# Another order for the first loads, splits and products of a Perceiver block on one Trainium2 core

## The chip, the core and the metric

The kernel runs on one core of one Trainium2 chip. The metric is the time of one execution on the device in microseconds (us), here the median of several runs.

## What is computed

The inputs are x (64 sequences of 64 rows, 256 wide) and a context (64 sequences of 256 rows, 256 wide). One block is applied to x:

```python
x = x + xattn(layernorm(x), ctx, ctx, Wq, bq, Wk, bk, Wv, bv, Wo, bo)   # 16 heads of 16
x = x + attn(layernorm(x), w_qkv, b_qkv, w_out, b_out)                  # causal, 16 heads
x = x + ffn(layernorm(x), w_gate, w_up, w_down)                         # quantized silu(gate)*up, inner 1024
```

In the cross attention, the only part that the change touches, `q = queries @ Wq.T + bq`, `k = keys @ Wk.T + bk`, `v = values @ Wv.T + bv`, then softmax of `q k / 4` over the 256 keys, times v, times Wo.

## The kernel before

Two sequences (2 x 64 rows of x) make one tile of 128 rows; there are 32 tiles, t = 0 to 31, and each has two contexts s = 0 and 1, one for each of its sequences. The program is written by hand for each engine, with semaphores between them. An engine runs its own list strictly in order, so the place of an instruction in its list decides what waits behind it. Three stages follow one another: cross attention for all tiles (to about 560 us), causal self attention, feed forward. The change lies ahead of the first loop of the first stage and in the first pass of it.

Products that need accuracy are split: a float32 matrix is copied to its float32r rounding ("h") by ScalarE, and the remainder ("l") is formed by a subtraction. The product is then three float32r products, h by h, h by l and l by h, each over two halves of the 256 inner values. So a key or value projection of one context is 12 matmuls of 128x256.

The pieces, by name and line:

- `pe_xt` (L269 to L275): two transposes of the normalized tile `xn` by TensorE. `act_xt` (L466 to L470) copies the result to `xnT` and rounds it to `x1h`; `pool_xl1` (L513 to L517) forms `x1l`.
- `pe_q` (L277 to L286): queries of two tiles at once, 12 matmuls whose moving side is 256 columns wide (2 x 128 rows of x). `dve_q` (L415 to L424) adds the bias and masks by head into `qb`, four instructions.
- `act_c` and `pool_c` split a context into `ch` and `cl`. `pe_k` (L288) and `pe_v` (L301) project it; `dve_k` (L410) and `dve_v` (L405) take the results out of PSUM and add the bias.
- `pe_scores` (L317) makes the scores of one context, 8 float32 matmuls on 32 rows each. `dve_max` (L456) takes the row maxima, `act_exp` (L492) the eight exponentials, `pe_transpose` (L335) 16 transposes of the probabilities, and `pe_pv` (L353) the product with the values. `pool_rm` and `pe_r` (L346) bring the reciprocal sums into place.
- `dve_stats` and `dve_xn` (L380 to L403) are the layer norm; POOL's `pool_rstd` (L511) sits between them. `pool_xb` (L519 to L522) adds the output bias to x into `x_all`.
- The weights `wk`, `wv`, `wq` are split once at the start: ScalarE makes `wkh`, `wvh`, `wqh` (L1472 to L1477), VectorE `wkl`, `wvl`, `wql` (L1309 to L1316).

SyncE's queue issues the loads of x and of the contexts. In `body(t)` it waits for `xn_done` t + 1 and `xb_done` t + 1 before it loads the x of tile t + 2, and behind that, in order, come the contexts of tile t + 1:

```python
sp_.wait_ge(xn_done, t + 1)
sp_.wait_ge(xb_done, t + 1)
sp_.dma_start(x_sb[j][:], x_v[bass.ds(t + 2, 1)].rearrange(
```

VectorE's `body(0)` begins with `dve_stats` of tile 2, which waits for that x. GpSimd's list at the start (L1594 to L1603) is `pool_rstd(0)`, `pool_c(0, 0)`, `pool_rstd(1)`, `pool_xl1(0)`, `pool_xl1(1)`, `pool_c(0, 1)`, `pool_xb(0)`, `pool_xb(1)`. ScalarE's `act_exp(0, 0)` stands behind `act_xt(1)` and `act_c(0, 1)` (L1478 to L1480).

Of the kernel before, what the change touches and what calls it, by code (L numbers as in the profile page):

```python
# [44 lines left out]
def block_kernel(nc, x, ctx_t, wq, bq, wk, bk, wv, bv, wo, bo, w_qkv, b_qk, b_v2, w_out, b_out,  # L45
# [8 lines left out]
    with ctx:  # L54
# [128 lines left out]
        wk_in = sem("wk_in")  # L183
        wv_in = sem("wv_in")
# [9 lines left out]
        SET_Q = [(wq_sb[:], k_of(wq)), (bq_sb[:], bq), (bk_sb[:], bk), (qm_sb[:], q_mask)]  # L194
# [23 lines left out]
        q_mm = sem("q_mm")  # L218
        qb_done = sem("qb_done")
# [36 lines left out]
        xt1_ps = mp[:, 0:D].rearrange("p (k t) -> p k t", k=KT)  # L256
# [12 lines left out]
        def pe_xt(pe, t, to):  # L269
            pe.wait_ge(xn_done, t + 1)  # L270
            if not isinstance(t, int) or t > 2:
                pe.wait_ge(y_ev, t - 2)
            for k in range(KT):
                last = nc.tensor.transpose(to[:, k, :], xn[:, k * P:(k + 1) * P], id_sb[:])
            last.then_inc(xt_mm, 1)  # L275

# [40 lines left out]
        def pe_scores(pe, t, s, n, j):  # L317
# [4 lines left out]
            for m in range(KT):  # L322
                pe.wait_ge(qb_done, n * 4 + 2 * m + 2)
# [91 lines left out]

        def dve_q(v, n):
# [48 lines left out]
        def act_xt(a, t, n, j, turned):  # L465
            a.wait_ge(xt_mm, t + 1)  # L466
            a.wait_ge(x1l_done, t)
            nc.scalar.activation(xnT[:], turned, ACT.Copy).then_inc(xt_ev, 1)
            a.wait_ge(q_mm, n)
            nc.scalar.activation(x1h[:, :, j * P:(j + 1) * P], turned, ACT.Copy).then_inc(x1h_done, 1)  # L470
# [619 lines left out]
        with nc.Block() as block:  # L1090
            @block.sync
            def _(sp_):
                sp_.dma_start(x_sb[0][:], x_v[0]).then_inc(x_in[0], 16)
                sp_.dma_start(c_sb[0][:], c_v[0, 0]).then_inc(c_in[0], 16)
                sp_.dma_start(x_sb[1][:], x_v[1]).then_inc(x_in[1], 16)
# [38 lines left out]
            def _(pe):  # L1134
                pe.wait_ge(id_in, 16)
                pe_xt(pe, 0, xt_ps)
                pe.wait_ge(wl_split, 1)
                pe_k(pe, 0, 0)
                pe_xt(pe, 1, xt1_ps)
                pe.wait_ge(wl_split, 2)  # L1140
                pe_v(pe, 0, 0)
                pe.wait_ge(wl_split, 3)
                pe_q(pe, 0)
                pe_scores(pe, 0, 0, 0, 0)

                def body(t, n, j, first=False, wsum=False, ahead2=True):
# [10 lines left out]
                    pe_pv(pe, t, 0, ahead2)  # L1157
                    if j == 1:
                        pe_q(pe, n + 1)
# [140 lines left out]
            def _(v):  # L1300
# [7 lines left out]
                dve_stats(v, LN1, 1, x_sb[1][:], (x_in[1], 16))  # L1308
                v.wait_ge(wh_split, 1)  # L1309
                nc.vector.tensor_tensor(wkl[:], wk_sb[:], wkh[:].bitcast(F32),  # L1310
                                        ALU.subtract).then_inc(wl_split, 1)
                dve_xn(v, LN1, 1, x_sb[1][:], xt_mm)
                for n, (w, h, l) in enumerate(((wv_sb, wvh, wvl), (wq_sb, wqh, wql))):
                    v.wait_ge(wh_split, n + 2)
                    nc.vector.tensor_tensor(l[:], w[:], h[:].bitcast(F32),
                                            ALU.subtract).then_inc(wl_split, 1)  # L1316
                v.wait_ge(wq_in, 16 * len(SET_Q))
                dve_k(v, 0, 0)
                v.wait_ge(w1_in, 16 * len(SET1))
                dve_v(v, 0, 0)  # L1320
                dve_q(v, 0)
                dve_max(v, 0, 0)

                def body(t, n, j, first=False, scale=False, piece=None, ahead2=True):
# [16 lines left out]
                    dve_max(v, t, 1)  # L1341
                    if j == 1:
                        dve_q(v, n + 1)
# [121 lines left out]
            def _(a):  # L1465
                a.dma_start(id_sb[:], ident).then_inc(id_in, 16)
                a.dma_start(wk_sb[:], k_of(wk)).then_inc(wk_in, 16)
                for dst, src in SET_Q:
                    a.dma_start(dst, src).then_inc(wq_in, 16)
# [3 lines left out]
                act_xt(a, 0, 0, 0, xt_ps)  # L1473
                a.wait_ge(wv_in, 16)
                nc.scalar.activation(wvh[:], wv_sb[:], ACT.Copy).then_inc(wh_split, 1)
                a.wait_ge(wq_in, 16 * len(SET_Q))
                nc.scalar.activation(wqh[:], wq_sb[:], ACT.Copy).then_inc(wh_split, 1)  # L1477
# [115 lines left out]
            def _(p):  # L1593
                p.wait_ge(const_set, 1)  # L1594
                pool_rstd(p, LN1, 0)
                pool_c(p, 0, 0)
                pool_rstd(p, LN1, 1)
                pool_xl1(p, 0, 0)
# [137 lines left out]
```

## Time and profile before

| | |
|---|---|
| median of 3 runs | 913.46 us (912.77 to 914.16) |
| the profiled execution, its own time | 913.29 us |
| its span (first to last instruction) | 911.5 us |
| mean granted TensorE clock in it | 0.997 |
| TensorE matmul busy | 875.0 us (96%) |
| VectorE busy | 758.0 us (83%) |
| ScalarE busy | 695.5 us (76%) |
| GpSimd busy | 431.4 us (47%) |

The span is 1.8 us shorter than the execution's own time, which holds a little ahead of the first and behind the last instruction. PE is TensorE, PEld its weight loads, DVE VectorE, ACT ScalarE, POOL GpSimd, SP SyncE; an engine's name with a q is its queue issuing a DMA. The busy share is a mean over stages; for a change at the start what counts is when TensorE gets to work without a break, and what it waits for until then. A matmul's own duration in the trace is longer than its share of TensorE's time, since matmuls overlap; the distance from start to start is the price.

### The profile page before, as it was taken

The page shows a single profiled execution, that of the slowest core. Times are in us where ns is not written, and L with a number is a line of the kernel's source. Part 1 is how long each engine was busy: PE and PEld are TensorE (multiplying, and loading weights), DVE is VectorE, ACT ScalarE, POOL GpSimd, SP SyncE. Part 2 cuts the span into 40 slices and gives each one's busy share as a digit, 9 for nine tenths or more (in the row PEclk, how much of TensorE's full clock was granted, in tenths as well). Part 3 has the DMA queues.
Part 4 walks back from the last instruction along what each step waited for, and adds up shares of the span by engine and source line. Part 5 has one row for each costly group of instructions (what it writes and reads, how often), then busy time and mean ns, then how long its engine had stood idle before and what let it go on. Part 6 is the DMA issues. An engine that isn't in the chain of part 4 may idle for free.

```text
span 911.5 us, 28303 instructions
## 1 busy us (share of the span) xinstructions
PE 875.0 (96%) x9650; PEld 732.8 (80%) x9666; DVE 758.0 (83%) x1587; ACT 695.5 (76%) x2046; POOL 431.4 (47%) x643
## 2 busy tenths in 40 slices
PE   6999999999999999999999997999999998999997
PEld 5888888888988888888889886888787886666664
DVE  5878878888888888877877876988888888999995
ACT  4777887776776777777777765777777778899996
POOL 3333333333233333333433327676666653677775
PEclk9999999999999999999999999999999999999999
DMA  6222111111110111111111100000000000001001
GB/s 183 96 88 82 41 46 30 42 49 29 41 46 29 41 46 39 31 46 41 32 43 40 35 2 1 3 2 0 1 0 0 0 3 2 23 31 36 29 33 37
DMA packets 31637, 31.86 MB, mean 35 GB/s; under 512 B 3280, under 2 KB 30800, under 8 KB 31568
## 3 DMA queue, kind: packets, MB, share of 16 engines
q1 hardware_dynamic: 30448, 30.47, 11.0%
q10 hardware_dynamic: 1120, 0.59, 0.2%
q8 instruction: 28, 0.46, 0.2%
q14 instruction: 41, 0.34, 0.1%
HBM read 26.86 MB, written 4.19 MB: 34 GB/s over the span
## 4 chain that ended last, share of the span: by engine, by line
PE 78%; ACT 12%; issue 4%; DVE 4%; DMA 0%; POOL 0%; ACTq 0%; DVEq 0%; SPq 0%; POOLq 0%
PE psum L342 11%; PE psum L297 9%; PE psum L329 9%; PE psum L312 9%; PE psum L368 6%; PE psum L665 5%; ACT probs L1017 4%; PE psum L703 3%; PE psum L714 3%; PE psum L377 3%; PE psum L284 3%; PE psum L750 3%; ACT probs L503 3%; PE psum L684 2%; PE psum L350 2%
## 5 line engine op out<-in xcount | busy, mean ns | idle before, releaser
L503 ACT ACTIVATE probs<-psum,nmax 128x256 f32<-128x256 f32 x512 | 237.3, 487 | 63.3 <-DVE nmax L460 62.4
L460 DVE TENSOR_REDUCE nmax<-psum 128x2 f32<-128x512 f32 x256 | 158.9, 683 | 24.3 <-PE psum L329 23.6
L511 POOL TENSOR_TENSOR rstd<-vare,minus_half 128x1 f32<-128x1 f32 x96 | 53.1, 553 | 153.8 <-DVE vare L398 151.3
L342 PE MATMUL psum<-id_sb,probs 128*128 128x128 f32 x1024 | 124.6, 273 | 0.5 <-ACT probs L503 0.5
L527 POOL TENSOR_TENSOR cl<-c_sb,ch 128x512 fp32r<-128x512 f32 x64 | 81.6, 1274 | 78.8 <-ACT ch L478 78.8
L342 PEld LDWEIGHTS psum<-id_sb,probs 128*128 128x128 f32 x1024 | 112.9, 140 | 3.4 <-ACT probs L503 2.8
L484 ACT ACTIVATE probsT<-psum 128x512 f32<-128x512 f32 x160 | 89.4, 603 | 30.7 <-PE psum L342 30.5
L503 ACT ACTIVATION_READ_ACCUMULATOR probs<-psum,nmax 128x1 f32 x512 | 112.6, 220 | 0.0
L534 POOL TENSOR_TENSOR rm<-rinv,hm_sb 128x256 f32<-128x256 f32 x64 | 39.7, 620 | 120.7 <-DVE rinv L437 120.7
L329 PE MATMUL psum<-k_sb,qb 32*128 32x256 f32 x1024 | 88.8, 401 | 3.8 <-DVE k_sb L413 1.8
L329 PEld LDWEIGHTS psum<-k_sb,qb 32*128 32x128 f32 x1024 | 62.1, 184 | 15.4 <-issue 10.8
L368 PE MATMUL psum<-probsT,v_sb 128*32 128x128 f32 x2048 | 69.2, 276 | 0.0
L368 PEld LDWEIGHTS psum<-probsT,v_sb 128*32 128x32 f32 x2048 | 52.0, 109 | 21.1 <-issue 20.7
L430 DVE COPY probsT<-psum 128x512 f32<-128x512 f32 x96 | 63.2, 658 | 0.3
L858 POOL TENSOR_TENSOR w_all<-c_sb,qm_sb 128x1024 f32<-128x1024 f32 x32 | 60.6, 1893 | 3.0 <-ACT c_sb L808 3.0
L444 DVE TENSOR_TENSOR o_prod<-psum,r_sb 128x256 f32<-128x256 f32 x64 | 27.0, 422 | 40.9 <-issue 34.9
L312 PE MATMUL psum<-wvh,ch 128*128 128x256 f32 x256 | 60.2, 317 | 0.0
L297 PE MATMUL psum<-ch,wkh 128*128 128x256 f32 x256 | 56.9, 304 | 2.2 <-DVE wkl L1310 1.6
L838 ACT ACTIVATE w_all<-w_all 128x1024 f32<-128x1024 f32 x32 | 33.9, 1058 | 27.4 <-DVE w_all L763 27.4
L408 DVE TENSOR_TENSOR v_sb<-psum,bv_sb 128x512 f32<-128x512 f32 x64 | 43.9, 686 | 11.9 <-PE psum L312 11.8
L297 PE MATMUL psum<-cl,wkh 128*128 128x256 f32 x256 | 51.7, 283 | 0.0
L297 PE MATMUL psum<-ch,wkl 128*128 128x256 f32 x256 | 51.3, 282 | 0.0
(141 smaller groups left out, 2334.9 us busy)
## 6 DMA issues: line engine op xcount, KB each, us to landing
c_sb<-in_ctx_t SPq DMA_DIRECT2D x64, 256.0 KB, 2.7
x_sb<-in_x SPq DMA_DIRECT2D x32, 128.0 KB, 2.4
out<-y_sb SPq DMA_DIRECT2D x32, 128.0 KB, 1.7
w_all<-in_w_gate SPq DMA_DIRECT2D x1, 1024.0 KB, 6.5
w_all<-in_w_up SPq DMA_DIRECT2D x1, 1024.0 KB, 5.7
w_all<-in_w_down SPq DMA_DIRECT2D x1, 1024.0 KB, 5.8
wqkv_sb<-in_w_qkv SPq DMA_DIRECT2D x1, 768.0 KB, 5.7
wk_sb<-in_wk ACTq DMA_DIRECT2D x1, 256.0 KB, 3.9
```

What stands on the lines that cost most here:

```text
L297: last = nc.tensor.matmul(k_ps[:, m, :], w[:, k, cols], c[s][:, k, :], start=n + k == 0, stop=n == 2 and k == KT - 1)
L312: last = nc.tensor.matmul(v_ps[:, kh, :], c[s][:, k, keys], w[:, k, :], start=n + k == 0, stop=n == 2 and k == KT - 1)
L329: last = nc.tensor.matmul(sp[c][:, m * S:(m + 1) * S], qb[m][rows, 2 * j + s, :, :].rearrange("p h q -> p (h q)"), k_sb[rows, m, :], start ...
L342: last = nc.tensor.transpose(sp[g][:, c:c + P], probs[:, 2 * g + u, kh * P:(kh + 1) * P], id_sb[:])
L368: last = nc.tensor.matmul(op[32 * c:32 * c + 32, m * P:(m + 1) * P], v_sb[s][:, kh, 32 * j:32 * j + 32], probsT[:, 2 * c + m, kh, :], star ...
L430: nc.vector.tensor_copy(probsT[:, 2 * g:2 * g + 2, :, :].rearrange("p a b c -> p (a b c)"), sp[g]).then_inc(pt_dve, 1)
L460: nc.vector.tensor_reduce(nmax[:, 2 * g:2 * g + 2], sp[g].rearrange("p (u s) -> p u s", u=2), AX.X, ALU.max, negate=True).then_inc(max_don ...
L484: nc.scalar.activation(probsT[:, 2 * g:2 * g + 2, :, :].rearrange("p a b c -> p (a b c)"), sp[g], ACT.Copy).then_inc(pt_act, 1)
L503: nc.scalar.activation(probs[:, j, :], sp[g][:, u * S:(u + 1) * S], ACT.Exp, bias=nmax[:, j:j + 1], accum_out=rsum[:, j:j + 1]).then_inc(e ...
L511: nc.gpsimd.tensor_tensor(rstd[:], vare[:], minus_half[:], ALU.pow).then_inc(ln.rstd_done, 1)
L527: nc.gpsimd.tensor_tensor(cl[s][:], c_sb[s][:], ch[s][:].bitcast(F32), ALU.subtract).then_inc(cl_done, 1)
L858: nc.gpsimd.tensor_tensor(kbd4[j][:], kT2[s][:, :, j * P:(j + 1) * P].unsqueeze(2).to_broadcast([P, KT, 4, P]), qm4_sb[:].unsqueeze(1).uns ...
```

## The change

On SyncE's queue wq is loaded third, ahead of the x of tile 1; ScalarE's queue loads the three small operands bk, bq and the mask alone, under a semaphore of their own (`b_in`). ScalarE runs an Exp on a 128x1 constant first. Queries of tile 0 are projected alone (`pe_q0(pe, 0)`, 128 columns) ahead of the first scores, those of tile 1 in the first pass (`pe_q0(pe, 1)`); the values of context (0, 0) and the transposes of tile 1 come behind the first scores. VectorE splits wk, wq, wv in this order. TensorE multiplies a tile of ones 8 times ahead of its first transposes and 4 times behind them; nothing reads these products. From tile 2 on `pe_q` and `dve_q` are as before.

```diff
-        SET_Q = [(wq_sb[:], k_of(wq)), (bq_sb[:], bq), (bk_sb[:], bk), (qm_sb[:], q_mask)]
+        SET_B = [(bk_sb[:], bk), (bq_sb[:], bq), (qm_sb[:], q_mask)]
...
-        xt1_ps = mp[:, 0:D].rearrange("p (k t) -> p k t", k=KT)
+        xt1_ps = op[:, 0:D].rearrange("p (k t) -> p k t", k=KT)
...
+        def pe_q0(pe, j):
+            pe.wait_ge(x1l_done, j + 1)
+            pe.wait_ge(qb0_done, j * 4)
+            at_t = slice(j * P, (j + 1) * P)
+            for m in range(KT):
+                cols = slice(m * P, (m + 1) * P)
+                for i, (w, x) in enumerate(((wqh, x1h), (wqh, x1l), (wql, x1h))):
+                    for k in range(KT):
+                        last = nc.tensor.matmul(q_ps[:, m, at_t], w[:, k, cols], x[:, k, at_t],
+                                                start=i + k == 0, stop=i == 2 and k == KT - 1)
+            last.then_inc((q0_mm, q_mm)[j], 1)
...
+        def dve_q0(v, j):
+            v.wait_ge((q0_mm, q_mm)[j], 1)
+            at_t = slice(j * P, (j + 1) * P)
+            for m in range(KT):
+                for h in range(2):
+                    nc.vector.tensor_scalar(
+                        qb[m][:, 2 * j:2 * j + 2, h, :],
+                        q_ps[:, m, at_t].rearrange("p (a q) -> p a q", a=2),
+                        bq_sb[:, m:m + 1], qm_sb[:, h:h + 1], ALU.add,
+                        ALU.mult).then_inc((qb0_done, qb_done)[j], 1)
...
                 sp_.dma_start(c_sb[0][:], c_v[0, 0]).then_inc(c_in[0], 16)
+                sp_.dma_start(wq_sb[:], k_of(wq)).then_inc(wq_in, 16)
                 sp_.dma_start(x_sb[1][:], x_v[1]).then_inc(x_in[1], 16)
...
+                pe.wait_ge(const_set, 2)
+                for i in range(8):
+                    nc.tensor.matmul(sp[0][:, 0:P], ones[:], ones[:], start=True, stop=True)
                 pe.wait_ge(id_in, 16)
                 pe_xt(pe, 0, xt_ps)
+                for i in range(4):
+                    nc.tensor.matmul(sp[0][:, 0:P], ones[:], ones[:], start=True, stop=True)
                 pe.wait_ge(wl_split, 1)
                 pe_k(pe, 0, 0)
+                pe.wait_ge(wl_split, 2)
+                pe_q0(pe, 0)
+                pe_scores(pe, 0, 0, 0, 0)
+                pe.wait_ge(wl_split, 3)
+                pe_v(pe, 0, 0)
+                pe.wait_ge(x1h_done, 1)
                 pe_xt(pe, 1, xt1_ps)
-                pe.wait_ge(wl_split, 2)
-                pe_v(pe, 0, 0)
-                pe.wait_ge(wl_split, 3)
-                pe_q(pe, 0)
-                pe_scores(pe, 0, 0, 0, 0)
...
                     pe_pv(pe, t, 0, ahead2)
+                    if first:
+                        pe_q0(pe, 1)
...
                     dve_max(v, t, 1)
+                    if first:
+                        dve_q0(v, 1)
...
-                for dst, src in SET_Q:
-                    a.dma_start(dst, src).then_inc(wq_in, 16)
+                for dst, src in SET_B:
+                    a.dma_start(dst, src).then_inc(b_in, 16)
+                a.wait_ge(const_set, 1)
+                nc.scalar.activation(nmr[:], minus_half[:], ACT.Exp)
                 act_c(a, 0, 0)
...
                 pool_c(p, 0, 0)
+                pool_xl1(p, 0, 0)
                 pool_rstd(p, LN1, 1)
-                pool_xl1(p, 0, 0)
                 pool_xl1(p, 1, 1)
                 pool_c(p, 0, 1)
```

TensorE's list from its beginning, before. `x1h` and `x1l` are the split queries' input, `ch` and `cl` the split context, `psum` every result.

```order
L274 MATMUL psum<-id_sb,xn 128x128 x2
...
L297 MATMUL psum<-ch,wkl 128x256 x2
L274 MATMUL psum<-id_sb,xn 128x128 x2
L312 MATMUL psum<-wvh,ch 128x256 x2
...
L312 MATMUL psum<-wvh,cl 128x256 x2
L284 MATMUL psum<-x1h,wqh 128x256 x2
...
L284 MATMUL psum<-x1h,wql 128x256 x2
L329 MATMUL psum<-k_sb,qb 128x256 x8
L297 MATMUL psum<-ch,wkh 128x256 x2
```

And in the changed kernel:

```order
L1173 MATMUL psum<-ones 128x128 x8
L277 MATMUL psum<-id_sb,xn 128x128 x2
L1177 MATMUL psum<-ones 128x128 x4
...
L313 MATMUL psum<-ch,wkl 128x256 x2
L289 MATMUL psum<-x1h,wqh 128x128 x2
...
L289 MATMUL psum<-x1h,wql 128x128 x2
L348 MATMUL psum<-k_sb,qb 128x256 x8
L328 MATMUL psum<-wvh,ch 128x256 x2
...
L328 MATMUL psum<-wvh,cl 128x256 x2
L277 MATMUL psum<-id_sb,xn 128x128 x2
L313 MATMUL psum<-ch,wkh 128x256 x2
```

The values and the transposes of tile 1 moved from ahead of the scores to behind them, and the query products became 128 columns wide.

VectorE's list from the first `xn` to the row maxima, before:

```order
L403 TENSOR_SCALAR xn<-x_sb,mv,rstd 128x256
L391 BN_STATS stat<-x_sb 128x6
L393 BN_AGGR mv<-stat 128x2
L398 TENSOR_SCALAR vare<-mv 128x1
L1310 TENSOR_TENSOR wkl<-wk_sb,wkh 128x512
L403 TENSOR_SCALAR xn<-x_sb,mv,rstd 128x256
L1315 TENSOR_TENSOR wvl<-wv_sb,wvh 128x512
L1315 TENSOR_TENSOR wql<-wq_sb,wqh 128x512
L413 TENSOR_TENSOR k_sb<-psum,bk_sb 128x512
L408 TENSOR_TENSOR v_sb<-psum,bv_sb 128x512
L421 TENSOR_SCALAR qb<-psum,bq_sb,qm_sb 128x4x64 x4
L460 TENSOR_REDUCE nmax<-psum 128x2 x4
```

And in the changed kernel:

```order
L422 TENSOR_SCALAR xn<-x_sb,mv,rstd 128x256
L1353 TENSOR_TENSOR wkl<-wk_sb,wkh 128x512
L1356 TENSOR_TENSOR wql<-wq_sb,wqh 128x512
L432 TENSOR_TENSOR k_sb<-psum,bk_sb 128x512
L410 BN_STATS stat<-x_sb 128x6
L412 BN_AGGR mv<-stat 128x2
L417 TENSOR_SCALAR vare<-mv 128x1
L440 TENSOR_SCALAR qb<-psum,bq_sb,qm_sb 128x2x64 x4
L422 TENSOR_SCALAR xn<-x_sb,mv,rstd 128x256
L1364 TENSOR_TENSOR wvl<-wv_sb,wvh 128x512
L490 TENSOR_REDUCE nmax<-psum 128x2 x4
L427 TENSOR_TENSOR v_sb<-psum,bv_sb 128x512
```

The second `xn` and the split `wvl` moved behind the four `qb` instructions, and the values' eviction behind the maxima.

## Rows read from the trace of the kernel before

**Rows 1.** The page, part 1: busy time, share of the span, instructions
```profile
PE 875.0 (96%) x9650; PEld 732.8 (80%) x9666; DVE 758.0 (83%) x1587; ACT 695.5 (76%) x2046; POOL 431.4 (47%) x643
```
**Rows 2.** The chain that ended last, 5 to 23 us: start, us, what
```profile
6.64 0.87 DVE wkl L1310
...
7.56 2.93 PE psum L297 x12
...
13.11 1.43 PE psum L284 x12
...
14.56 1.91 DVE qb L421 x4
...
18.03 3.76 ACT probs L503 x16
```
**Rows 3.** Timeline, ScalarE at the start: start, us, engine, line [idle before <-releaser]
```profile
3.68 1.28 ACT L478 ACT_TABLE_LOAD   x1 [3.68 <-issue]
...
8.45 0.63 ACT L1477 ACTIVATE wqh<-wq_sb 128x512 fp32r<-128x512 f32 x1 [0.83 <-DMA qm_sb<-in_q_mask]
```
**Rows 4.** Timeline, ScalarE's queue; and DMA issues, 0 to 1.7 us, with us to landing
```profile
1.67 0.50 ACTq L1469 DMA_DIRECT2D wq_sb<-in_wq  x1
...
wq_sb<-in_wq ACTq DMA_DIRECT2D x1, 256.0 KB, 4.8
```
**Rows 5.** Timeline, the ones, from which the filler products read
```profile
0.86 0.17 DVE L1302 MEMSET ones<- 128x128 f32 x1
```
**Rows 6.** Timeline, from the transposes of tile 1 to the second context's remainder
```profile
10.28 0.63 PE L274 MATMUL psum<-id_sb,xn 128*128 128x128 f32 x2
...
12.44 1.28 POOL L527 TENSOR_TENSOR cl<-c_sb,ch 128x512 fp32r<-128x512 f32 x1
...
17.16 0.50 PE L297 MATMUL psum<-ch,wkh 128*128 128x256 f32 x2
```
**Rows 7.** The chain: the transposes and the output product in later passes
```profile
28.45 1.75 PE psum L342 x16
...
37.51 0.86 PE psum L377 x4
```
**Rows 8.** Timeline and tile x_sb, 14 to 16 us: how x of tile 2 comes
```profile
13.68 1.43 POOL L522 TENSOR_TENSOR x_all<-x_sb,bo_sb 128x256 f32<-128x256 f32 x2
...
14.51 0.33 SPq L1106 DMA_DIRECT2D x_sb<-in_x  x1
...
DMA to landing us min/median/max: 2.1/2.1/2.1
```
**Rows 9.** Timeline, VectorE from tile 2's statistics to TensorE's transposes of it
```profile
19.65 0.41 DVE L391 BATCH_NORM_STATS2 stat<-x_sb 128x6 f32<-128x256 f32 x1
...
21.82 0.20 DVE L437 RECIPROCAL rinv<-rsum 128x8 f32<-128x8 f32 x1 [0.69 <-ACT probs L503]
...
22.49 0.41 DVE L403 TENSOR_SCALAR xn<-x_sb,mv,rstd 128x256 f32<-128x256 f32 x1
...
23.04 0.38 PE L274 MATMUL psum<-id_sb,xn 128*128 128x128 f32 x2
```
**Rows 10.** Timeline, where the key products of tile 1 begin
```profile
24.71 1.27 POOL L527 TENSOR_TENSOR cl<-c_sb,ch 128x512 fp32r<-128x512 f32 x1 [1.22 <-ACT ch L478]
...
25.63 0.44 PE L350 MATMUL psum<-id_sb,rm 128*128 128x128 f32 x2
...
26.08 0.48 PE L297 MATMUL psum<-ch,wkh 128*128 128x256 f32 x2
```
**Rows 11.** Timeline, the 12 query products inside a pass, 256 columns wide
```profile
41.56 0.50 PE L284 MATMUL psum<-x1h,wqh 128*128 128x256 f32 x2
...
43.09 0.38 PE L350 MATMUL psum<-id_sb,rm 128*128 128x128 f32 x2
```
**Rows 12.** Windows near 565 us: busy by engine, granted clock, DMA share, GB/s; and timeline
```profile
566.00:568.00 2.00, 2.00 (x19) 1.06 (x12) 0.81 (x3) 0.25 (x1) 1.61 (x3) 0.50 0.00 0
...
565.13 0.39 PE L696 MATMUL psum<-ca_b,id_b 64*128 64x512 bf16 x2 [2.12 <-ACT ch L800]
```

More of the change, by code:

```diff
@@ L183, in block_kernel @@
         wk_in = sem("wk_in")
+        b_in = sem("b_in")
         wv_in = sem("wv_in")
@@ L218, in block_kernel @@
         q_mm = sem("q_mm")
+        q0_mm = sem("q0_mm")
+        qb0_done = sem("qb0_done")
         qb_done = sem("qb_done")
@@ L322, in pe_scores @@
             for m in range(KT):
-                pe.wait_ge(qb_done, n * 4 + 2 * m + 2)
+                if isinstance(t, int) and t == 0:
+                    pe.wait_ge(qb0_done, 2 * m + 2)
+                else:
+                    pe.wait_ge(qb_done, n * 4 + 2 * m + 2)
                 for c in range(4):
@@ L468, in act_xt @@
             nc.scalar.activation(xnT[:], turned, ACT.Copy).then_inc(xt_ev, 1)
-            a.wait_ge(q_mm, n)
+            if isinstance(t, int) and t == 2:
+                a.wait_ge(q0_mm, 1)
+            else:
+                a.wait_ge(q_mm, n)
             nc.scalar.activation(x1h[:, :, j * P:(j + 1) * P], turned, ACT.Copy).then_inc(x1h_done, 1)
@@ L1307, in _ @@
                 dve_xn(v, LN1, 0, x_sb[0][:], xt_mm)
-                dve_stats(v, LN1, 1, x_sb[1][:], (x_in[1], 16))
                 v.wait_ge(wh_split, 1)
@@ L1311, in _ @@
                                         ALU.subtract).then_inc(wl_split, 1)
-                dve_xn(v, LN1, 1, x_sb[1][:], xt_mm)
[L1313 to L1318, printed above, removed]
+                v.wait_ge(wh_split, 2)
+                nc.vector.tensor_tensor(wql[:], wq_sb[:], wqh[:].bitcast(F32),
+                                        ALU.subtract).then_inc(wl_split, 1)
+                v.wait_ge(b_in, 16 * len(SET_B))
+                dve_k(v, 0, 0)
+                dve_stats(v, LN1, 1, x_sb[1][:], (x_in[1], 16))
+                dve_q0(v, 0)
+                dve_xn(v, LN1, 1, x_sb[1][:], xt_mm)
+                v.wait_ge(wh_split, 3)
+                nc.vector.tensor_tensor(wvl[:], wv_sb[:], wvh[:].bitcast(F32),
+                                        ALU.subtract).then_inc(wl_split, 1)
+                dve_max(v, 0, 0)
                 v.wait_ge(w1_in, 16 * len(SET1))
                 dve_v(v, 0, 0)
-                dve_q(v, 0)
-                dve_max(v, 0, 0)
                 def body(t, n, j, first=False, scale=False, piece=None, ahead2=True):
@@ L1473, in _ @@
                 act_xt(a, 0, 0, 0, xt_ps)
+                a.wait_ge(wq_in, 16)
+                nc.scalar.activation(wqh[:], wq_sb[:], ACT.Copy).then_inc(wh_split, 1)
                 a.wait_ge(wv_in, 16)
                 nc.scalar.activation(wvh[:], wv_sb[:], ACT.Copy).then_inc(wh_split, 1)
-                a.wait_ge(wq_in, 16 * len(SET_Q))
-                nc.scalar.activation(wqh[:], wq_sb[:], ACT.Copy).then_inc(wh_split, 1)
                 act_xt(a, 1, 0, 1, xt1_ps)
```

## The prediction, made before the changed kernel ran

> **What bounds the kernel now.** I read the busy shares first, then the chain that ended last, then the timeline of each engine up to 45 us. TensorE is busy for 875 of 911.5 us [rows 1]: once it runs without a break, a microsecond added to its list is a microsecond of the end, and a microsecond that another engine saves is worth nothing. The change can only pay in what TensorE waits for at the start, so I look for the point from which it never waits again. The chain shows it: VectorE's split of wk ends and the first key products start at 7.56 us, then come values, queries (13.11), VectorE's four `qb` instructions (14.56), the scores, and ScalarE's eight exponentials from 18.03 to 21.79 [rows 2]. The last group of transposes waits for the last exponential; behind that every link of the chain is TensorE.
>
> A second thing is to be seen in these rows. The 12 key products from 7.56 us take 2.93 us with the transposes' start behind them, and the 12 query products from 13.11 take 1.43 us, though they have the same shape [rows 2]: 0.24 against 0.12 us each. TensorE had been busy without a break from 7.56 on when its rate doubled near 12.3 us, so these are its 1.2 and 2.4 GHz levels, though the granted clock in the windows reads 1.00 throughout. Where a matmul below is priced warm it is 0.118 us for a 128x256 float32r product.
>
> **The start, step by step.** *ScalarE.* Its queue issues one load fewer, so the table load moves from 3.68 to about 3.2 us. It already ran right behind the queue's last issue, not behind data [rows 3]; "loaded on a constant" by itself brings nothing, and costs one tiny Exp, which I estimate at 0.2 us (bounds: 0, and the 0.47 us, 3.76 / 8, of a 128x256 Exp [rows 2]). So the context and wk are rounded 0.25 us earlier. *VectorE* no longer has tile 1's statistics ahead of `wkl`, which starts near 6.0 instead of 6.64 and takes 0.87 [rows 2]: key products from about 6.9 us instead of 7.56.
>
> *The fillers.* They can start behind the ones [rows 5], at about 1.1 us. A 128x256 float32 product costs 0.43 us warm (0.86 us for two, each in two parts [rows 7]), so one of 128 columns 0.215 warm, 0.43 at the lower level. Eight end at about 4.5 us, ahead of the first transposes; the four behind these take 0.9 to 1.7 us and end between 6.5 and 7.7. They are free if TensorE has its full rate by then, and cost up to 0.8 us if not. I take the rate as full from about 6.5 us, since TensorE now works nearly without a break from 1.1 us on; at the latest that I allow, 9 us, everything up to the first pass is 1.1 us later than below.
>
> *Keys and queries.* 12 x 0.118 = 1.42: keys 6.9 to 8.3. wq is issued at about the same moment as before (1.67 us), on the other queue, and lands 4.8 us later, at 6.5 [rows 4]; its rounding was held until 8.45 by the mask's load under the common semaphore [rows 3] and now runs at 6.5, so `wql` is ready at 8.0 and not in the way. The query product of one tile is the first unknown: 12 products whose moving side is 128 columns. The trace has no float32r product that narrow. Bounds: half of the 256-wide one, 0.059 us; and the float32 price above, 0.215. I take 0.118, the price of the same instruction with the same 128 columns of weights: the transposes, also 128 wide with weights of their own, need 1.75 / 16 = 0.109 us [rows 7], nearly as much as a product of twice the width, so width alone doesn't set it. Queries 8.3 to 9.75, their results at 9.9.
>
> The Trainium skill has two rules on this ("TensorE: Matmul & The Clock Gate"). Under "LDWEIGHTS (loading the stationary operand)" a load takes its columns divided by 1.2 GHz, 107 ns for 128, and the trace agrees, by the transposes' 0.109 [rows 7]. Under "Back-to-back issue gap" a stream of weight loads and products of 128 columns is measured at about 81 ns each; by that the 24 products would cost 0.9 us less than I take, and the sum would end near no change. No row here shows 81 ns.
>
> *Evictions.* The four `qb` instructions took 1.91 us at 256 columns [rows 2]; at 128 they take between half and all of that, and I take 1.2 us (a fixed part stays): 10.0 to 11.2. Scores run meanwhile, to 12.0. Behind `qb` on VectorE stand `xn` of tile 1 and `wvl`, 0.35 and 0.6 us: ready at 12.2. **Only then** can TensorE start the values (12.25 to 13.7), and behind them the transposes of tile 1 at 13.7. From the start of these to the end of `cl` of context (0, 1) before lie 13.72 - 10.28 = 3.44 us [rows 6], through ScalarE's two copies and its rounding of the context and POOL's two subtractions; at full rate 0.2 less. So `cl` ends at 16.95, and the key products of (0, 1) start at 17.0 us. Before, they started at 17.16 [rows 6]. All that was gained at the start is spent by this row of dependences. The exponentials do start earlier, near 15.3 instead of 18.03, and end near 19.1.
>
> *From there.* TensorE's work up to the end of the transposes is 18 x 0.118 + 1.75 = 3.87 us; it now finds every exponential ready and is done at 20.9, where it was done at 22.5. But what it meets next is the transposes of tile 2, which need tile 2's x. SyncE loads that only after POOL's first addition to `x_all`, and this stands behind `cl` of (0, 1) in POOL's list. Before: 13.68 + 0.72, issue at 14.51, landed 2.1 us later [rows 8], with 3 us to spare. Now: 16.95 + 0.72 + 0.1 + 2.1 = 19.9. VectorE's list is stopped there. From the statistics to the end of `xn` it needs 22.90 - 19.65 less the 0.69 us that it waited for ScalarE, 2.56 us [rows 9]: 22.45, transposes at 22.55 instead of 23.04. That is what is left of the gain: **0.5 us**, with TensorE idle for 0.9.
>
> *The first pass.* Tile 1's query products now lie between the product with the values and `pe_r`, in TensorE's unbroken stretch. Twelve such products of 256 columns cost 43.09 - 41.56 = 1.53 us there [rows 11]; by the choice above I take **1.5 us** (bounds: 0.7 at half price, 2.7 at the float32 price). VectorE's four extra `qb` instructions, 1.2 us, lie beside these products. The key products of tile 1 waited 0.25 us for `cl` before (they started 0.45 us behind `pe_r`, 0.1 behind the end of `cl` at 25.98 [rows 10], where 0.2 behind `pe_r` is usual); that wait is gone: **0.25 us** back.
>
> *The clock.* TensorE will be idle near 10 us for 0.9, and from 14.0 to 17.0 for 3 us. Later in this kernel it waits 2.12 us with little to do on either side, and the granted clock is then 0.50 over two microseconds, the 1.2 GHz level [rows 12]. If it falls here, the keys, values and transposes that follow run at the lower level; 0.9 us of that is covered by the wait for tile 2. I price it at 0 to 0.9 us and take 0.25.
>
> **The sum**: -0.5 + 1.5 - 0.25 + 0.25 = +1.0 us on the profiled execution's 913.29, 914.3; the median of the runs is 0.17 above that execution, so 914.5.
>
> **Rivals.** *A, narrow float32r products cost what float32 does.* At 0.215 the twelve at the start end 1.2 us later and all behind them moves, since x of tile 2 hangs on them; the twelve in the pass cost 1.2 more. +1.0 + 2.4 = +3.4, 916.8; with the spread of the clock 915.6 to 917.6. For it: no float32r product of this trace is narrower than 256, so no row speaks against it, and the float32 row is about as near as the one I took. It decides as soon as a product costs over 0.151 us, where the sum passes 1.8. This is the slower side.
>
> *B, narrow products cost half, 0.059.* 0.7 less in each place: -0.4, 913.0; 912.4 to 913.5 with the other choices. Against it: the transposes' 0.109.
>
> *C, the start carries through.* TensorE meets the first pass at 17.0 without the 1.5 us of waits for the exponentials, and if x of tile 2 were not late, that would all be gain: -1.6 + 1.25 = -0.4, again 913.0, and only with B's price -1.8. The profile speaks against it, as POOL's and SyncE's lists put that load behind `cl`.
>
> *D, the fillers do not raise the rate.* Keys start at 7.7 and run slowly: +1.1 more, 915.6.
>
> **How the numbers follow.** Differences under 0.2%, 1.8 us, can't be told from no change here. Forecast (with D's part of it) 0.45, 913.6 to 915.6; A 0.43; B or C 0.12. Slower by over 0.2% means over 915.3: 0.15 of the forecast, 0.9 of A, together 0.455. Faster by that much means under 911.6: only B and C together, 0.04. The rest is 0.505. For 8 in 10 the range leaves out the lower half of B and C and the top of A: 912.9 to 917.2.
>
> **What would show it.** Right: key products of (0, 1) at about 17.0 us behind POOL's `cl`; VectorE idle in front of tile 2's statistics, released by the x load near 19.9; TensorE waiting about 0.9 us for tile 2's `xn`; a dozen query products in the pass from start to start in 1.5 us. A would show as 2.6 us there and `qb` at 11 instead of 10. Wrong: exponentials no earlier than 17 (the start failed), statistics of tile 2 not waiting for x (then C), or a span that changed behind 60 us.

## The result and the profile after

The changed kernel takes 916.47 us, median of 8 runs (915.73 to 918.96), where the kernel before takes 914.15 (8 runs beside it, 912.77 to 915.70). The ratio is 1.0027, 95% interval 1.0016 to 1.0038: slower by 0.27%. Two executions that took far longer than all the others, 1669.77 us of the kernel before and 2115.19 us of one experiment, are left out of the ratios below and of that experiment's median. The profiled execution took 916.86 us, its span is 915.0 (before 913.29 and 911.5). From the profile's page, busy time and count of each engine:

```profile
PE 880.8 (96%) x9686; PEld 740.0 (81%) x9702; DVE 757.6 (83%) x1591; ACT 695.6 (76%) x2047; POOL 431.7 (47%) x643
```

The chain of the changed kernel over the first 29 us, start, duration, what:

```profile
6.07 1.34 PE psum L1177 x8
7.41 1.70 PE psum L313 x12
...
10.62 1.34 DVE qb L440 x4
11.96 0.32 DVE xn L422
12.28 0.61 DVE wvl L1364
12.89 0.04 issue
12.94 1.68 PE psum L328 x12
14.61 0.23 PE psum L277 x2
...
15.15 0.38 ACT x1h L503
15.53 0.53 ACT ch L511
16.05 1.66 issue
17.71 2.90 PE psum L313 x12
...
26.33 1.49 PE psum L289 x12
27.82 0.25 PE psum L369 x2
28.07 0.94 PE psum L313 x8
```

The fillers do their work: the first twelve key products take 1.70 us with their tail where they took 2.93 [rows 2]. Then the row of dependences of the prediction is there link by link (`qb`, `xn`, `wvl`, values, transposes of tile 1, ScalarE, POOL under the word "issue"), and the key products of context (0, 1) start at 17.71 us, 0.55 later than before [rows 6], and run slowly: 2.70 us from the start of the first to the start of what follows (20.41), where the first twelve take 1.52. The timelines of VectorE and POOL, with idle time and releaser behind each row:

```profile
6.01 1.35 DVE L1353 TENSOR_TENSOR wkl<-wk_sb,wkh 128x512 fp32r<-128x512 f32 x1 [0.75 <-ACT wkh L1523]
...
21.06 0.43 DVE L410 BATCH_NORM_STATS2 stat<-x_sb 128x6 f32<-128x256 f32 x1 [5.19 <-DMA x_sb<-in_x]
```

```profile
5.53 1.27 POOL L560 TENSOR_TENSOR cl<-c_sb,ch 128x512 fp32r<-128x512 f32 x1 [0.72 <-ACT ch L511]
...
16.35 1.26 POOL L560 TENSOR_TENSOR cl<-c_sb,ch 128x512 fp32r<-128x512 f32 x1
17.57 1.41 POOL L555 TENSOR_TENSOR x_all<-x_sb,bo_sb 128x256 f32<-128x256 f32 x2
```

VectorE stood idle for 5.19 us in front of tile 2's statistics, released by the load of x, as forecast, but at 21.06 us, where 19.9 was forecast. The transposes of tile 2 start at 23.64 (before 23.04 [rows 9]), tile 1's queries and the keys behind them like this:

```profile
26.26 0.44 PE L289 MATMUL psum<-x1h,wqh 128*128 128x128 f32 x2
26.54 0.39 PE L289 MATMUL psum<-x1l,wqh 128*128 128x128 f32 x2
...
27.65 0.42 PE L369 MATMUL psum<-id_sb,rm 128*128 128x128 f32 x2
27.83 0.36 PE L313 MATMUL psum<-ch,wkh 128*128 128x256 f32 x1
```

Tile 1's key products start 1.75 us later than before (27.83 against 26.08 [rows 10]). The stretches of the changed kernel in which the clock was lower, the columns being us, busy time and count of PE, PEld, DVE, ACT, POOL, then the granted clock and DMA:

```profile
17.10:22.50 5.40, 4.79 (x31) 4.82 (x32) 1.31 (x5) 2.82 (x13) 2.35 (x4) 0.68 0.43 124
553.10:556.40 3.30, 3.30 (x18) 3.30 (x17) 1.14 (x6) 0.84 (x2) 1.40 (x1) 0.50 0.02 5
570.10:573.50 3.40, 3.40 (x19) 3.16 (x16) 2.31 (x2) 1.19 (x2) 3.15 (x3) 0.50 0.00 0
```

Before had one such stretch in its profile, from 565.5 to 568.9 us [rows 12], and the last 1.3 us of its span; in the changed kernel it is the last 0.2 us. To see where the 3.57 us of the two profiled executions lie I compare the start of the same pass in both: the changed kernel is behind by 1.77 us at 37 us, 2.13 at 88, 2.26 at 122, 2.24 to 2.27 from 223 us to 541, 3.78 at 559, 3.34 at 573, 3.62 at 779. So 1.77 are of the start; 0.5 arise in three steps between 64 and 142 us (0.38, 0.13 and 0.12, of which 0.17 come back at 217), which nothing in the change explains at sight, and 1.5 come with the fall of the clock at 553. How many falls an execution has differs from run to run: the runs' mean clocks are 0.992 to 0.995, those of before mostly 0.996 or 0.997. Start and steps make 2.3 us, the difference of the medians.

### The profile page after: what moved, and what is told of

Same layout as the page of the kernel before. It is cut to its first block, busy times and chain, and to the rows that moved or that the text cites. A ratio compares the mean times of both kernels' runs of the same rounds, so it can differ in the third digit from the quotient of the medians.

```text
span 915.0 us, 28381 instructions
## 1 busy us (share of the span) xinstructions
PE 880.8 (96%) x9686; PEld 740.0 (81%) x9702; DVE 757.6 (83%) x1591; ACT 695.6 (76%) x2047; POOL 431.7 (47%) x643
## 4 chain that ended last, share of the span: by engine, by line
PE 79%; ACT 12%; issue 4%; DVE 3%; POOL 0%; DMA 0%; DVEq 0%; ACTq 0%; POOLq 0%
PE psum L361 11%; PE psum L313 9%; PE psum L348 9%; PE psum L328 9%; PE psum L387 6%; PE psum L698 5%; ACT probs L1050 4%; PE psum L736 4%; PE psum L747 4%; PE psum L396 3%; PE psum L783 3%; PE psum L300 3%; PE psum L717 3%; ACT probs L536 2%; PE psum L369 2%
## 5 line engine op out<-in xcount | busy, mean ns | idle before, releaser
L490 DVE TENSOR_REDUCE nmax<-psum 128x2 f32<-128x512 f32 x256 | 158.8, 682 | 23.4 <-PE psum L348 22.7
```

The costliest lines, as they stand in the source:

```text
L490: nc.vector.tensor_reduce(nmax[:, 2 * g:2 * g + 2], sp[g].rearrange("p (u s) -> p u s", u=2), AX.X, ALU.max, negate=True).then_inc(max_don ...
```

## The experiments

**No fillers.** The twelve products of ones at the start are left out.

```
-                for i in range(8):
-                    nc.tensor.matmul(sp[0][:, 0:P], ones[:], ones[:], start=True, stop=True)
...
-                for i in range(4):
-                    nc.tensor.matmul(sp[0][:, 0:P], ones[:], ones[:], start=True, stop=True)
```

> The changed kernel without the 12 products of ones. If the fillers are what brings TensorE to its full rate by 7.4 us: the first key products start at about 7.4 us all the same (wkl ends then), but keys and queries run at half rate, 2.5 + 2.4 us instead of 2.8 together, and the key products of tile 1 start about 2 us later than in the changed kernel (27.8 us), near 29.8; time 1 to 2 us longer. If the fillers only delay (they end at 7.4): the same start or 0.1 to 0.3 us earlier, and no longer time.

920.75 us (5 runs), ratio 1.0050 (1.0031 to 1.0068).

```profile
7.55 0.79 PE L313 MATMUL psum<-ch,wkh 128*128 128x256 f32 x2 [1.65 <-DVE wkl L1349]
8.14 0.63 PE L313 MATMUL psum<-cl,wkh 128*128 128x256 f32 x2
...
19.64 0.76 PE L313 MATMUL psum<-ch,wkh 128*128 128x256 f32 x2 [2.88 <-issue]
...
30.96 0.36 PE L313 MATMUL psum<-ch,wkh 128*128 128x256 f32 x1
```

The first twelve key products start at 7.55 us and take 2.73 us, where they take 1.52 with the fillers. D falls: they do raise the rate. Everything is late by 1.9 us at the keys of (0, 1) and by 3.1 at tile 1's, so without fillers the change would have cost 4.9 us at this point. Both this and the median, 4.3 us above the changed kernel's, are more than I expected (2 us and 1 to 2): the granted clock was 0.50 from 18.68 to 25.51 us, twice as long as in the changed kernel.

**The gap filled.** Twelve products of ones behind the transposes of tile 1, where TensorE waits for `cl`.

```
                 pe_xt(pe, 1, xt1_ps)
+                for i in range(12):
+                    nc.tensor.matmul(mp[:, 0:P], ones[:], ones[:], start=True, stop=True)
```

> The changed kernel with 12 more products of ones behind tile 1's transposes, in TensorE's idle stretch from 14.7 to 17.7 us. Theory of two limits that end together (lower clock, late x of tile 2): the granted clock stays 1.00 from 17 to 22.5 us, keys of (0, 1) take 1.4 instead of 2.9 us, but TensorE then waits for tile 2's xn until 23.5, and tile 1's keys start at 27.6 to 27.8 as in the changed kernel (27.83). Rival, the lower clock is the loss: tile 1's keys start 1.4 us earlier, at 26.4.

**x of tile 2 early.** POOL adds to `x_all` before it makes `xl` of tile 1 and `cl` of (0, 1), so that SyncE may load tile 2's x.

```
+                p.wait_ge(w1_in, 16 * len(SET1))
+                for j in range(2):
+                    pool_xb(p, j, 0, j)
                 pool_xl1(p, 1, 1)
                 pool_c(p, 0, 1)
-                p.wait_ge(w1_in, 16 * len(SET1))
-                for j in range(2):
-                    pool_xb(p, j, 0, j)
```

> The changed kernel with POOL's two additions to x_all ahead of x1l of tile 1 and cl of (0, 1), so that x of tile 2 is loaded about 6 us earlier (near 12 us instead of 18.4) and lands by 15. Theory of two limits: VectorE no longer waits 5.2 us for x, but the granted clock falls as before, TensorE's work fills the time to 23.8, and tile 1's keys start within 0.3 us of 27.8. Rival, the late x is the loss: they start about 1.3 us earlier, at 26.5.

**Both.**

> Both together. Theory of two limits: now tile 1's keys start about 1.4 us earlier than in the changed kernel, at 26.4, which is 0.3 us behind the kernel before (26.08), and the time falls by 1.4 us, from about 2.3 us above before to about 1. If a third wait stands behind them (the eviction of k, cl of tile 1): less than 0.7 us earlier.

Gap filled: 916.97 us (10 runs), ratio 1.0022 (1.0011 to 1.0033). x early: 917.45 (10), 1.0028 (1.0019 to 1.0038). Both: 915.87 (10), 1.0013 (1.0001 to 1.0024). From the windows and TensorE's timeline of the first, then of both:

```profile
17.10:22.50 5.40, 5.01 (x42) 4.65 (x40) 2.12 (x7) 3.57 (x14) 2.82 (x5) 1.00 0.61 160
```

```profile
17.50 0.47 PE L313 MATMUL psum<-ch,wkh 128*128 128x256 f32 x2 [0.21 <-issue]
...
22.78 0.44 PE L277 MATMUL psum<-id_sb,xn 128*128 128x128 f32 x2 [0.45 <-DVE xn L422]
...
27.01 0.48 PE L313 MATMUL psum<-ch,wkh 128*128 128x256 f32 x2
```

```profile
17.95 0.48 PE L313 MATMUL psum<-ch,wkh 128*128 128x256 f32 x2 [0.21 <-issue]
...
22.62 0.38 PE L277 MATMUL psum<-id_sb,xn 128*128 128x128 f32 x2
...
26.58 0.48 PE L313 MATMUL psum<-ch,wkh 128*128 128x256 f32 x2
```

From the keys of (0, 1) to those of tile 1 before needs 8.92 us, the changed kernel 10.12, the filled gap 9.51, x early alone 10.20, both 8.63. With x early, the clock costs 1.57 us (10.20 against 8.63); with the clock up, the late x costs 0.88 (9.51 against 8.63). They are two limits that end together: in the changed kernel `xn` of tile 2 is ready at 23.53 us, and the slow products let TensorE start on it at 23.64.

The 0.6 us that the filled gap gains is neither theory's number (tile 1's keys start at 27.01, between 26.4 and 27.6 to 27.8), and it is not the clock's price: the load of x landed 2.05 us after its issue there and 2.66 after it in the changed kernel, which is the same 0.6, and TensorE waited for `xn` all the same (0.45 in the second row). Why the load took longer in one profile than in the other stays open. In the medians the filled gap gained nothing. Both together came near to what was expected: tile 1's keys at 26.58 us (26.4), and a median 1.3 us above before (about 1).

The test of x early alone is weak. The clock fell there from 13.74 to 17.16 us, which made the start worse by itself, and again from 20.57 to 23.98, so that 3.41 us at the lower clock lie inside the 10.20, and 2.83 inside the 10.12 of the changed kernel.

**Tile 1's queries in the gap**, real work in place of the fillers; without and with x early.

```
                 pe_xt(pe, 1, xt1_ps)
+                pe_q0(pe, 1)
...
                 dve_v(v, 0, 0)
+                dve_q0(v, 1)
...
-                    if first:
-                        pe_q0(pe, 1)
-                    if first:
-                        dve_q0(v, 1)
```

> The changed kernel with tile 1's query products taken out of the first pass and put behind its transposes, ahead of the keys of (0, 1); their eviction behind that of the values. If the 1.4 us of products in the pass are a term of the loss of their own, the way from the keys of (0, 1) to the keys of tile 1 shortens by 1.4 us (10.1 in the changed kernel; 8.7 here, 0.6 less if the clock does not fall). If x of tile 2 is a limit of its own it stays at 9.4 to 9.5 less 1.4, that is 8.1 or more. Time 1.0 to 1.5 us below the changed kernel.

> The same, with POOL's two additions early as in xb_early. Without the late x the same way takes 8.6 - 1.4 = 7.2 us where the clock stays (8.7 if it falls), tile 1's keys start near 25.2, 0.9 us ahead of the kernel before (26.08): time level with before or 1 us below.

916.80 us (9 runs), ratio 1.0028 (1.0019 to 1.0038), and 916.04 (9), 1.0012 (0.9996 to 1.0028). A miss: the queries need `xl` of tile 1 and start in the first at 17.76 us, at the end of the gap. TensorE is as idle as before, and its clock falls from 13.1 to 16.5 and from 19.9 to 23.4 us in the first profile, from 13.4 to 23.6 in the second. The second version took 913.5 to 913.8 us in the four runs whose mean clock was 0.997, and 916 to 920 in those at 0.994 and less: how much of the time the clock is down moves the time more than this order does.

**Context (0, 1) first.** On top of x early, ScalarE rounds the context ahead of tile 1's copies, POOL makes `cl` first and `xl` of tile 1 last, and tile 1's queries stand behind the first half of the values of (0, 1), their eviction by VectorE behind that of the keys.

```
-                act_xt(a, 1, 0, 1, xt1_ps)
                 act_c(a, 0, 1)
+                act_xt(a, 1, 0, 1, xt1_ps)
...
                     pe_v(pe, t, 1, (0,))
+                    if first:
+                        pe_q0(pe, 1)
                     pe_transpose(pe, t, 0)
```

> A version that should beat both kernels: context (0, 1) is rounded ahead of tile 1's transposes (ScalarE is idle from 8.8 us), its remainder and the additions to x_all are formed by POOL ahead of x1l of tile 1, and tile 1's query products lie between the values of (0, 1) and the transposes, where TensorE would wait for exponentials. My theory says that the idle 3 us exist only through the order of ScalarE's and POOL's lists: the keys of (0, 1) then start at about 14.7 instead of 17.7 us, the clock does not fall, and tile 1's keys start near 23.4, 2.7 us ahead of the kernel before; ratio to before 0.997. Rival, the loads or the exponentials hold it: they start at 25 or later, ratio 0.999 to 1.001.

**Exponentials first.** As the last, but ScalarE's exponentials stand ahead of tile 1's copies and tile 1's queries are left where the change has them.

> As c01_q1, but the eight exponentials stand ahead of tile 1's copies on ScalarE, and tile 1's query products are left in the first pass. Exponentials from 13.5 instead of 15.9 us, transposes end near 17.8 instead of 19.8; the query products cost 1.4 in the pass: tile 1's keys at 22.6 to 23.0, 3 us or more ahead of before, ratio 0.9965. If ScalarE's late copies of the probabilities (behind tile 1's copies) hold the next scores: 23.5 or later.

915.84 us (12 runs), ratio 1.0015 (1.0005 to 1.0025), and 915.07 (12), 1.0010 (1.0001 to 1.0019). The first has its keys of (0, 1) at 15.81 us, tile 1's at 25.02, so 1.06 us ahead of before (I had expected 2.7: the values wait until 14.15 for `wvl`, 1.21 us long beside POOL's additions). Yet its median is 1.3 us above that of the kernel before beside it (914.55): in its profile the clock was low from 548.1 to 555.0 and from 568.6 to 572.0 us, and the three steps cost their 0.5. Its lead of 0.61 us at 541 was a lag of 2.07 at 556: what the start gave, the clock took 500 us later.

Exponentials first missed as well. I had expected tile 1's keys at 22.6 to 23.0 us, and they start at 26.26, 0.18 behind before. The granted clock was 0.50 from 12.08 to 18.90 us in its profile, over the values and most of the keys of (0, 1), so this run does not tell what the order by itself is worth.

**The late gaps filled**, in the kernel before and in the changed one: 12 products of ones ahead of the first keys of the second attention, where TensorE waits near 547 us for POOL's remainder `cl` of the second attention, and 8 ahead of its passes, meant for the wait of [rows 12].

```
                 pe.wait_ge(qb_done, 2 * NT)
+                for i in range(12):
+                    nc.tensor.matmul(mp[:, 0:P], ones[:], ones[:], start=True, stop=True)
                 pe_k2(pe, 0, 0)
...
+                for i in range(8):
+                    nc.tensor.matmul(vp[:, 0:P], ones[:], ones[:], start=True, stop=True)
                 for t in range(4):
                     body2(t, t // 2, t, first=t == 0)
```

> The kernel before, its first 540 us untouched, with 12 products of ones in TensorE's idle stretch near 547 us and 8 in the one near 563. Two questions. If the clock's fall there costs what the traces show (it fell near 565 in the profile of before and near 553 and 570 in that of the change), the granted clock stays 1.00 from 540 to 580 us and the median falls by 1 to 2 us against before; if the stretches are limited by other engines, no change. And the first stage shows once more when its passes run: if the 0.46 us by which the change and seven other kernels lag behind the profile of before from 88 to 223 us is chance of that one profile, it shows here too.

> The changed kernel with the same 20 products. If the loss of the change lies in its first 28 us alone, the distance to before_late is that of the first passes, 1.7 to 2.3 us. If the change also makes the falls of the clock near 553 us more frequent by itself, the distance is smaller here than between the plain kernels (2.3 us).

916.09 us (12 runs), ratio 1.0011 (1.0002 to 1.0019), and 919.82 (7), 1.0062 (1.0040 to 1.0084): 1.6 us above the kernel before, where 1 to 2 below were expected. The first 12 lie in their gap and cost nothing: the keys behind them are 0.09 us behind the kernel before, their predecessors were 0.25. The 8 are misplaced: they stand behind the wait instead of in it, and delay the scores by 2.0 us. TensorE's timeline, the gap in the kernel before and then the filled kernel:

```profile
549.68 0.47 PE L665 MATMUL psum<-ch,w2h 128*128 128x256 f32 x2 [2.91 <-POOL cl L851]
```

```profile
562.63 0.44 PE L656 MATMUL psum<-id_sb,xn 128*128 128x128 f32 x2
565.19 2.05 PE L1250 MATMUL psum<-ones 128*128 128x128 f32 x16 [2.12 <-ACT ch L800]
```

In this profile the granted clock was 1.00 up to the end of the span, and of the 2.0 us 1.4 were back at 573: one fall costs about 1.5 us. But only two of the 12 executions had a mean clock of 1.0 (the profiled one is among them), and they took 913.95 and 914.19 us; the ten others had 0.998 and took 915.3 to 916.5. The fillers did not keep every fall away, and where the falls of those ten lie no trace shows.

In the changed kernel the same stretch had a clock of 1.00 too, and 1.4 of the 2.0 us were back. It is 3.7 us behind the filled kernel before all the same, where 1.7 to 2.3 were expected. In its profile 3.5 of them are there at 37 us already, as the clock was low at the start from 17.5 to 24.3 us.

**All together**: context (0, 1) first, the late fillers, and 4 products of ones on either side of the first scores.

```
                 pe_q0(pe, 0)
+                for i in range(4):
+                    nc.tensor.matmul(sp[0][:, 0:P], ones[:], ones[:], start=True, stop=True)
                 pe_scores(pe, 0, 0, 0, 0)
+                for i in range(4):
+                    nc.tensor.matmul(mp[:, 0:P], ones[:], ones[:], start=True, stop=True)
```

> c01_q1 with these 20 products, and 4 more ahead of the first scores and 4 behind them, where TensorE waits for VectorE. c01_q1 reached tile 1's keys 1.1 us ahead of the kernel before (25.0 against 26.1). Expected: the same here, granted clock 1.00 from 10 to 25 us and from 540 to 580, median 1.5 to 3 us below before, ratio 0.997 to 0.9985. If the fillers delay (contention on TensorE's queue): tile 1's keys at 25.5 or later and no better than before_late.

915.13 us (11 runs), ratio 1.0004 (0.9995 to 1.0013), the same as before, where 1.5 to 3 us less were expected, with the 2.0 us of the misplaced eight in it. The clock was 1.00 throughout in its profile (the mean clock was 1.0 in two of the 11 executions and 0.998 in nine), and the lead over before 1.28 us at 37 us, but only 0.83 at 223. The three steps between 64 and 142 us are in every version of the changed kernel so far. They are not in the kernel before with its late gaps filled, which falls behind before by 0.02 us at 37, 0.06 at 122 and, in small amounts, 0.25 at 541. The chain of the changed kernel at the first of them, then that of before at the same place:

```profile
72.56 0.88 PE psum L396 x4
73.43 0.03 issue
73.46 0.06 DVEq L484
73.53 0.42 issue
73.94 0.44 DVE x_all L484
74.38 0.14 issue
74.51 0.41 PE psum L277 x2
```

```profile
70.81 0.87 PE psum L377 x4
71.68 0.70 PE psum L312 x6
72.38 0.02 issue
72.40 0.41 PE psum L274 x2
```

VectorE adds tile t's output product to `x_all` 0.42 us late, with its own issue as the only cause that the chain shows, and the transposes of tile t + 2, which use the same bank, wait for it. At 107.6 and 141.2 us it is 0.17. These are the three rounds of VectorE's first loop, and the change had put three to four more instructions ahead of that loop (the pages count x1591 for VectorE against x1587).

**The loop back in its place.** As the last, without the misplaced eight, and with three memsets of constants, which nothing in the first stage reads, moved behind VectorE's second loop.

```
                 nc.vector.memset(ones[:], 1.0).then_inc(const_set, 1)
-                nc.vector.memset(v2[:], 0.0).then_inc(const_set, 1)
-                nc.vector.memset(eps_col[:], EPS).then_inc(const_set, 1)
-                nc.vector.memset(minus_one[:], -1.0).then_inc(const_set, 1)
...
+                nc.vector.memset(v2[:], 0.0).then_inc(const_set, 1)
+                nc.vector.memset(eps_col[:], EPS).then_inc(const_set, 1)
+                nc.vector.memset(minus_one[:], -1.0).then_inc(const_set, 1)
                 body(NT - 2, NT // 2 - 1, 0, ahead2=False)
```

> The run best without its 8 products ahead of the second attention's passes, and with three constants' memsets on VectorE (first used after the first stage) moved from the start of its program to behind its second loop. In the changed kernel's profile the passes lose 0.38, 0.13 and 0.12 us against before at 73.9, 107.6 and 141.2 us (0.17 comes back later): each time the output addition on VectorE (L484) starts 0.42, 0.17 and 0.17 us after what it waits for, its own issue being all that the chain shows, and in the first of them an instruction transfer is under way. The same three stand in best at 70.5, 104.4 and 138.0, and none in before or before_late. They are the three rounds of VectorE's first loop, whose place in its program the change moved by 3 to 4 instructions. Theory P, the loop's place in the program sets them: with three instructions taken away ahead of it the gaps are gone, and the lead over before stays what it is at 37 us, about -1.3, to the end of the first stage (best: -1.28 at 37, -0.84 from 223 on). Theory Q, they come from when the instructions run, or from the loads: the gaps stay and the lead falls to about -0.85. For the rest: the gap near 547 us is filled as in best, the 2.1 us wait at 565 is open again as in before, and a clock fall there as likely. Without the 2.0 us that the misplaced products cost, the end is 912.8 by P or 913.3 by Q where before gives 914.1; 1.5 us more for each clock fall more.

911.38 us (6 runs, 910.58 to 912.25), ratio 0.9967 (0.9954 to 0.9979): 0.33% faster than before (median 914.74 beside it). Its chain at the place, and two windows:

```profile
69.48 0.87 PE psum L396 x4
70.34 0.70 PE psum L328 x6
71.05 0.02 issue
71.07 0.41 PE psum L277 x2
```

```profile
17.10:22.50 5.40, 5.40 (x49) 5.06 (x52) 4.25 (x13) 4.61 (x18) 2.16 (x4) 1.00 0.77 259
...
557.00:575.00 18.00, 14.64 (x159) 11.59 (x150) 15.40 (x30) 11.32 (x28) 14.08 (x18) 1.00 0.01 2
```

The gaps are gone and the lead holds: 1.33 us at 37, 1.49 at 223, 1.60 at 559. P is shown, Q falls: up to 64 us TensorE's passes start within 0.06 us of where they did in the version with the gaps. The distance to before, 3.4 us, is 2 us more than P's 1.3. The fall of the clock near 565 stayed away in this profile, which is 1.5 of them; in the other runs that took about as long (910.6 to 910.7 us, mean clock 0.999 to 1.0) it can only be supposed. The three slower ones took 912.0 to 912.3 at 0.997 or 0.998, still 2.6 us less than before.

## Why the prediction was off

The forecast was 914.5 with "no change" as likeliest; 916.47 lies inside 912.9 to 917.2, but on the slower side, and not by the mechanism that I had given that side. The range reached so far up only for the sake of A, which is refuted, so that it held the result is in part luck.

*Right.* The price of a narrow query product: 12 in 27.65 - 26.26 = 1.39 us, forecast 1.5. A and B are refuted. By the Trainium skill's 81 ns ("TensorE: Matmul & The Clock Gate", "Back-to-back issue gap") the twelve would take 0.97, and the trace does not agree. The wait of tile 1's keys for `cl` is gone (0.18 us behind `pe_r` for 0.45), 0.27 back for 0.25. The fillers raise the rate before the first keys. The gain at the start is spent by the row through `qb`, `wvl` and tile 1, and x of tile 2 is late behind POOL's `cl`, both as worked out: C is refuted. One of the signs that I had named did not come: TensorE did not wait 0.9 us for tile 2's `xn`. It got there at 23.64, when `xn` had been ready for 0.1 us.

*The step that failed: "-0.5, what is left of the gain".* It became +0.6 (transposes of tile 2 at 23.64 us, not 22.55). Three terms of that row were too small. `wkl` took 1.35 us, not 0.87, and the keys started at 7.41, not 6.9; the four `qb` instructions took 1.34, not 1.2; by tile 1's transposes the row was 0.75 us late (14.45 for 13.7), and `cl` ended at 17.61, not 16.95. x of tile 2 landed 2.66 us after its issue at 18.38, not 2.1. With these, statistics came at 21.06, not 19.9. For `wkl` the reason can be read: I took its duration from a row in which it ran beside POOL's `cl` for 0.3 us only, and moved it to where it did for 0.8. For the load it can't: with the gap filled it was issued at nearly the same time (18.18) and landed after 2.05 us.

*The clock, mis-sized the other way.* It fell where I said, at 17.13, and was back at 20.54. I took 0.25 us for it; without the fall TensorE could have begun tile 2's transposes 0.1 us sooner at most, since `xn` ended at 23.53. It hid behind the late x, and x behind it; with x early it is worth 1.57. So the start cost 0.6 + 1.4 - 0.3 = 1.7 us, not 1.0.

*Not seen at all.* The prediction said a span that changed behind 60 us would prove it wrong, and it did change: +0.5 by the three rounds of VectorE's loop. I had counted what the four extra `qb` instructions cost where they run, and not that instructions ahead of a loop can slow the loop. These 0.5 and the 0.7 by which the start cost more than forecast are what took the result over the 0.2% line. Another fall near 550 us, 1.5 us, is in the profiled execution; how often it comes differs between runs of one kernel, and what sets that stays open.

## What to carry to other kernels

A reordering of a start is worth only what reaches the first unbroken stretch of the bounding engine: follow the row of dependences to there, and then ask which load is issued behind it. Where a gap in TensorE's work can't be closed, put products without use ahead of the wait, not behind it, and look at the granted clock over every gap of the whole program. When a pass deep in the kernel slows down after an edit far ahead of it, look for "issue" in the chain inside a loop, and try moving a few instructions across it.

## What was not expected of the hardware

*Code position.* Three to four VectorE instructions more ahead of a loop cost 0.42 us in its first round and 0.17 in each of the two others; with three taken away, nothing. An instruction queue moved 0.02 MB just then in the changed kernel, from 73 to 74 us:

```profile
q8 instruction: 1, 0.02, 7.1%
```

One also lies at 70 us in the last experiment, without a gap, so a transfer alone does not make one. Nor does every gap have one: in the changed kernel this queue moved nothing from 86 to 161 us, and the gaps at 107.6 and 141.2 lie there. The Trainium skill ("Runtime: NRT & Kernel Launch", "Instruction fetch mechanics") says that an engine's instructions come in blocks of 16 KiB, 256 of them, and that a taken branch to a block not held stalls it. The size agrees for queue 8 (28 transfers, 0.46 MB, by the profile) and not for the other instruction queue, 14 (41 transfers, 0.34 MB), and the profile does not say which engine a queue feeds. That a block's border in the loop is the cause was not shown; what is shown is that the place of the code decides.

*VectorE beside POOL.* `wkl`, a subtraction of two tensors in SBUF, took 0.86 us before [rows 2] and 1.35 here, while POOL made `cl` from 5.53 to 6.80. In the experiment with context (0, 1) first the like-sized `wvl`, 0.68 us long here, took 1.21 beside POOL's additions. POOL is slower too: `x1l` took 1.05 us beside `wkl` and `wql` here, and 0.72 by itself at 15.67. But VectorE does not always lose: with x early, `wvl` took 0.68 us beside POOL's second addition, and that addition 1.50 instead of 0.72.

*The clock.* The falls (17.13 to 20.54, 553.02 to 556.43 and 570.09 to 573.50 us in the changed kernel, 565.48 to 568.89 before) are at granted clock 0.50, the 1.2 GHz level: the twelve key products of (0, 1) take 2.70 us, the first twelve 1.52. One gap does not fix their place: with x early, the same order of work on TensorE, it fell at 13.7 us, and single runs of one kernel differ by a fall. With the gaps near 11, 13, 15 and 547 us closed or shortened it stayed at 1.00 in both profiles taken, at the start and around 550 us, though the mean clock was 0.997 or 0.998 in 12 of the 17 executions of these two versions; this, with the code position and context (0, 1) first, made the only version that is faster than before. Which of the three gives how much of the 3.4 us between the medians was not separated further than above.
